# First norm's factor moved to the outputs of the query, key and value projections, rotary swap by DMA

## The chip, the cores and the metric

The kernel runs on one core of a Trainium2 chip. The metric is the device time of one execution in microseconds (us). The engines are TensorE (PE, with its weight loads PEld), VectorE (DVE), ScalarE (ACT), GpSimd (POOL) and SyncE (SP). ACT and SP also issue DMAs, each on a queue of its own.

## The reference

The program is a chain of four cross-attention layers on x of 8 batches x 112 tokens x 512. All that concerns this change is the start of layer 0: an RMS norm, query, key and value projections with two sets of weights that a token mask chooses between, rotary position encoding, and self-attention in 16 heads of 32.

```
xn = ln_in_w * (x * rsqrt(mean(x*x) + 1e-6))
m  = (type[t] == 1) & (type[t+1] == 1)             # 0 for the last token
qkv = m * (xn @ v_qkv) + (1 - m) * (xn @ l_qkv)    # [.., 1536]
rotate_half(u) = concat(-u[16:32], u[0:16])        # within each head of 32
q, k = u * cos[pos] + rotate_half(u) * sin[pos]    # for u = q, k
self-attention (causal), dense, residual; cross-attention, gated MLP, and three more layers
```

A factor that belongs to one token can be put behind a projection, since the projection sums over features only.

## The kernel before

Activations are kept transposed, 128 features in the partitions by tokens in the columns; the 896 tokens are two halves of 448 (`HALF`), and 512 features are four blocks (`KD`). A float32 product is made of three passes in the fast format float32r: high by high, high by low and low by high. So each weight chunk of 128x1024 is loaded by SP into `raw` (3 slots), and split by GpSimd into `wh` (one copy) and `wl` (four subtractions), in 4 slots. A chunk of the stage `qk` holds the v and the l weights of one output block m, and there are 16 tiles in `RAW`'s order: half 0 with m 0 to 3, half 1 with m 0 to 3, then the same with m 4 to 7. m below 4 is q, above is k. One tile is 24 matmuls, 12 into each of two PSUM banks (`e` = 0 for v, 1 for l weights). A slot of `wh` is free once half 1's tile has used it.

The order of work on each engine is written out by hand. Each engine walks through `SEQ["qk"]`: norm steps `("norm", nn, half, part)`, the table step and the tiles. `PoolPlan` gives each PE tile a PSUM bank from a rotating list (3 banks before), and PE waits for the bank's last reader.

The head: ACT squares x (L998), DVE sums the squares into `total` (L1289, L1292), PE multiplies by 1/512 (L618), ACT takes the root (L1003), DVE the reciprocal (L1316) and x times weight times factor (L1331), ACT rounds that to `nh` (L1015), DVE subtracts to get `nl` (L1338). PE makes the cos and sin tables by a one-hot product (L628). The half 1 norm is hooked behind tile 0 (`s`) and tile 1 (`v`, `f`).

A tile's way out: DVE multiplies each bank by its mask and scale (L1529, twice), adds the two (L1562). PE then makes the swapped copy by a float32 matmul with `rot_w` (L913, two passes), one tile later. DVE's `rope` multiplies raw by cos (L1545), the swapped bank by sin (L1548), and adds (L1551). Behind the 16th tile PE computes the values projection of batch 0 (L874 to L876); ACT waits for all 16 ropes before it scales that (L1123), and DVE adds its part (L1412); then attention starts with scores (L802) and masked minimum (L1434).

Of the kernel before, what the change touches and what calls it, by code (L numbers as in the profile page):

```python
# [29 lines left out]
F32 = mybir.dt.float32  # L30
# [7 lines left out]
P = 128  # L38
SCRATCH = 1024
B, S, D = 8, 112, 512  # L40
T = B * S
# [112 lines left out]
LATE = (1, 2)  # L154
# [57 lines left out]
def build(nc, xT, ctxF, ctxK, kmask, tt, ttT, pos, walls, vecs, gates, consts, outT):  # L212
    ctx = ExitStack()
    with ctx:
# [50 lines left out]
        ctxt = at("ctxt", [P, 4, CH * CC], F32, o_k)  # L265
        rt = at("rt", [P, T], F32, o_k)
        vr2 = at("vr2", [P, 2, HALF], F32, o_k + 4 * T)
        place[0] = max(place[0], o_k + 4 * 4 * CH * CC)
# [35 lines left out]
        eps = sb("eps", [P, 2])  # L304
        o_a = place[0]
# [45 lines left out]
        raw_qk = sem("raw_qk")  # L351
        tile_ready = sem("tile_ready")
# [27 lines left out]
        gated = sem("gated")  # L380
        normed = sem("normed")
# [73 lines left out]
        def both(*hooks):  # L455
# [7 lines left out]
            "qk": [("norm", 0, 0, "s"), ("norm", 0, 0, "v"), ("table",), ("norm", 0, 0, "f")] + qk_order(parts(0, 1, s=(0, 0, 0), v=(0, 0, 1), f=(0, 0, 1))),  # L463
# [17 lines left out]
        for name in SEQ:  # L481
            for it in SEQ[name]:
                if it[0] == "norm" and it[3] in ("a", "s", "s0", "x", "x0"):
# [69 lines left out]

        block = ctx.enter_context(nc.Block())
# [3 lines left out]
        def _(pe):  # L558
# [49 lines left out]
            def norm_part(nn, half, part):  # L608
# [6 lines left out]
                elif part == "v":  # L615
                    n = begin_tile(("var", nn, half), "act")
                    pe.wait_ge(summed_up, sum_no[nn, half, "v"])
                    nc.tensor.matmul(pool_bank(n)[:, 0:HALF], mean_w, total[:, :], start=True, stop=True)\  # L618
                        .then_inc(tile_ready, 1)

            qk_seen = [0]
# [9 lines left out]
            def stage(name, rhs_of, nblocks, who, mpc, ready=None, nn=None, items=None, only=None):  # L631
# [10 lines left out]
                for j in items or range(len(seq)):  # L642
# [261 lines left out]
            pe.wait_ge(cst_in, 16)  # L904

            def nhl(half, i):
                return nh_[:, i, hcols(half)], nl_[:, i, hcols(half)]

            def rotate(i):

                pe.wait_ge(raw_qk, i + 1)
                n = begin_tile(("rot", i), "dve")
                nc.tensor.matmul(pool_bank(n)[:, 0:HALF], rot_w, scr[:, i % 2, :],  # L913
                                 start=True, stop=True).then_inc(tile_ready, 1)

# [5 lines left out]

            stage("qk", nhl, KD, ("dve", "dve"), 1, nn=0)
            rotate(len(RAW) - 1)


# [3 lines left out]

            attention(att_self)  # L930
# [32 lines left out]
        def _(act):  # L963
# [10 lines left out]
            def norm_part(nn, half, part):  # L974
# [24 lines left out]
                elif part == "v":  # L999
                    bank = empty(("var", nn, half))  # L1000
                    if turn_of[nn, half] >= 1:
                        act.wait_ge(std_used, turn_of[nn, half])
                    nc.scalar.activation(std[:, :], bank[:, 0:HALF], ACT.Sqrt,  # L1003
                                         bias=eps[:, 0:1] if e == 1e-6 else eps[:, 1:2]).then_inc(emptied["act"], 1)
# [13 lines left out]
            def stage(name, each):  # L1018
                for it in SEQ[name]:
                    if it[0] == "norm":  # L1020
                        norm_part(*it[1:])
                    elif it[0] == "table":
                        for i, dst in enumerate((cosT, sinT)):
                            bank = empty(("table", i))
                            nc.scalar.copy(dst[:, :], bank[:, 0:S]).then_inc(emptied["act"], 1)
# [79 lines left out]
            for half in range(2):  # L1105
                act.dma_start(x[:, :, hcols(half)], xT[:, :, hcols(half)]).then_inc(x_in[half], 16)
# [6 lines left out]
            act.wait_ge(vmT_done, 2)  # L1113
# [109 lines left out]
        def _(dve):  # L1223
# [22 lines left out]
            def norm_part(nn, half, part):  # L1246
# [13 lines left out]
                elif part in X_PART:  # L1260

                    if part in ("x", "x0"):
# [3 lines left out]
                    for k in X_PART[part]:  # L1266
# [3 lines left out]
                            .then_inc(normed, 1)  # L1270
                        dve.wait_ge(sq_ready, i + k + 1)
# [6 lines left out]
                    if part in ("x", "x3"):  # L1278
# [24 lines left out]
                elif part[0] in "rf" and nn in LATE:  # L1303
                    tile_done(dve, ("var", nn, half))
                    own = rt[:, cols] if nn == 2 else rstd[:, :]
# [612 lines left out]
```

## Time and profile before

| what | value |
|---|---|
| median of 3 runs | 2025.97 us (2022.82 to 2027.89) |
| profiled execution | 2026.49 us, its span 2024.5 us |
| PE busy | 1915.1 us, 95% |
| DVE busy | 1131.6 us, 56% |
| ACT busy | 831.1 us, 41% |
| POOL busy | 883.7 us, 44% |
| chain of waits | PE 82%, DVE 7%, POOL 5%, ACT 2%, issue 2% |
| DMA to landing, weight chunk of 512 KB | 3.6 us (median) |
| DMA sizes at the start | x 896 KB a half, constants 383.5 KB, token types 448 KB, positions 49 KB, vectors 26 KB |

Shares are averages over stages with different limits. The rows give start and duration in us from the span's start; a bracket at the end of a row is idle time of the engine before it and what ended it. `x4` at the end of a timeline row means that four alike were merged. The granted clock is a share of TensorE's full speed: 1.00 is 2.4 GHz, 0.50 is 1.2 GHz.

### The profile page before, as it was taken

What the parts mean: (1) busy time and instruction counts of PE and PEld (TensorE: products, weight loads), DVE (VectorE), ACT (ScalarE), POOL (GpSimd) and SP (SyncE); (2) the same over time, 40 slices, a digit from 0 to 9 for tenths busy, and PEclk for the clock granted to TensorE, in tenths of its full rate; (3) what the DMA queues carried; (4) which work ended last, traced back from release to release, by engine and by line L of the source; (5) the groups of instructions that cost most, each with busy time, mean ns of one, the idle gap of its engine ahead of it and who ended that gap; (6) DMA issues with size and microseconds to landing.
All of it is one profiled execution on the core that took longest, in us unless ns stands there. A gap on an engine that the chain in (4) does not pass through costs nothing.

```text
span 2024.5 us, 35457 instructions
## 1 busy us (share of the span) xinstructions
PE 1915.1 (95%) x12620; PEld 1643.0 (81%) x12620; DVE 1131.6 (56%) x2699; ACT 831.1 (41%) x2198; POOL 883.7 (44%) x1037
## 2 busy tenths in 40 slices
PE   4999989997999999999999999998979999999998
PEld 3776777776999989888988879985458988888997
DVE  6777866665543654547676554222384766655422
ACT  2017527884211211256666423222235666652321
POOL 3340313240888999642121338850044212104884
PEclk9999988998999999999999999999989999999999
DMA  3110100010333333310000123322221000001332
GB/s 127 42 58 2 40 16 17 30 54 3 96 113 106 114 114 115 98 35 18 10 24 12 55 76 105 105 83 88 76 75 35 18 10 24 13 1 42 105 115 78
DMA packets 38189, 118.87 MB, mean 59 GB/s; under 512 B 6168, under 2 KB 10264, under 8 KB 38016
## 3 DMA queue, kind: packets, MB, share of 16 engines
q1 hardware_dynamic: 31408, 107.92, 17.2%
q10 hardware_dynamic: 6608, 8.68, 1.4%
q8 instruction: 104, 1.70, 0.4%
q14 instruction: 69, 0.57, 0.1%
HBM read 114.75 MB, written 1.84 MB: 58 GB/s over the span
## 4 chain that ended last, share of the span: by engine, by line
PE 82%; DVE 7%; POOL 5%; ACT 2%; issue 2%; DMA 1%; DVEq 0%; ACTq 0%; SPq 0%; POOLq 0%
PE psum L580 15%; PE psum L582 14%; PE psum L581 14%; PE psum L802 7%; PE psum L813 6%; PE psum L860 5%; PE psum L573 4%; PE psum L700 4%; PE psum L702 4%; PE psum L701 4%; POOL wl L1760 3%; ACT probs_t L1067 1%; POOL wh L1752 1%; PE psum L874 1%; DVE rstd L1316 1%
## 5 line engine op out<-in xcount | busy, mean ns | idle before, releaser
L1760 POOL TENSOR_TENSOR wl<-raw,wh 128x256 fp32r<-128x256 f32 x656 | 512.5, 812 | 13.7
L1752 POOL TENSOR_SCALAR wh<-raw 128x1024 fp32r<-128x1024 f32 x164 | 189.5, 1155 | 402.0 <-PE psum L582 161.1
L580 PE MATMUL psum<-nh,wh 128*128 128x448 f32 x904 | 349.6, 387 | 14.2 <-DVEq L1531 5.3
L581 PE MATMUL psum<-nl,wh 128*128 128x448 f32 x904 | 337.0, 373 | 0.0
L582 PE MATMUL psum<-nh,wl 128*128 128x448 f32 x904 | 336.7, 372 | 0.0
L1067 ACT ACTIVATE probs_t<-masked_t,nmin 112x375 f32<-112x375 f32 (+1 forms) x384 | 202.6, 528 | 109.7 <-DVE nmin L1434 109.7
L1607 DVE TENSOR_TENSOR hid_l<-scr,hid_h 128x448 fp32r<-128x448 f32 x108 | 92.3, 855 | 227.7 <-ACT hid_h L1153 227.1
L580 PEld LDWEIGHTS psum<-nh,wh 128*128 128x128 f32 x904 | 175.0, 194 | 37.1 <-issue 13.3
L1434 DVE CUSTOM_DVE_ANT_0 masked_t<-psum,maskf 112x375 f32<-112x375 f32 x256 | 129.8, 545 | 116.6 <-PE psum L802 116.0
L1094 ACT COPY probsT_t<-psum 125x336 f32<-125x336 f32 (+1 forms) x424 | 175.4, 456 | 43.5 <-PE psum L860 24.3
L813 PE MATMUL psum<-cst,probs_t 112*125 112x112 f32 (+1 forms) x1304 | 189.7, 276 | 3.6 <-ACT probsT_t L1094 3.2
L581 PEld LDWEIGHTS psum<-nl,wh 128*128 128x128 f32 x904 | 175.0, 194 | 20.0 <-issue 5.5
L813 PEld LDWEIGHTS psum<-cst,probs_t 112*125 112x125 f32 (+1 forms) x1304 | 167.0, 186 | 25.5 <-issue 9.3
L582 PEld LDWEIGHTS psum<-nh,wl 128*128 128x128 f32 x904 | 174.2, 193 | 15.0
L1474 DVE TENSOR_SCALAR probs_t<-probs_t,rinv 112x376 f32<-112x376 f32 (+1 forms) x392 | 157.8, 444 | 7.2
L1752 POOL TENSOR_SCALAR ctxh<-raw 128x750 fp32r<-128x750 f32 x24 | 20.1, 837 | 324.2 <-PE psum L582 206.8
L700 PE MATMUL psum<-hid_h,wh 128*128 128x448 f32 x432 | 157.8, 365 | 0.0
L702 PE MATMUL psum<-hid_h,wl 128*128 128x448 f32 x432 | 157.2, 364 | 0.0
L701 PE MATMUL psum<-hid_l,wh 128*128 128x448 f32 x432 | 157.2, 364 | 0.0
L1053 ACT COPY v<-psum 125x512 f32<-125x512 f32 (+1 forms) x144 | 68.6, 477 | 124.0 <-PE psum L860 119.0
L1168 ACT ACTIVATE scr<-psum 128x448 f32<-128x448 f32 x64 | 34.9, 545 | 199.9 <-PE psum L582 184.8
L860 PE MATMUL psum<-probsT_t,v 125*64 125x112 f32 (+1 forms) x2304 | 113.5, 264 | 1.3 <-ACT probsT_t L1094 1.1
(192 smaller groups left out, 3874.1 us busy)
## 6 DMA issues: line engine op xcount, KB each, us to landing
raw<-in_walls SPq DMA_DIRECT2D x183, 512.0 KB, 3.6
raw<-in_ctxF SPq DMA_DIRECT2D x24, 375.0 KB, 3.0
ctxb<-in_ctxF ACTq DMA_DIRECT2D x8, 375.0 KB, 3.5
ctxt<-in_ctxK ACTq DMA_DIRECT2D x8, 375.0 KB
x<-in_xT ACTq DMA_DIRECT2D x2, 896.0 KB, 11.5
outT<-x SPq DMA_DIRECT2D x2, 896.0 KB, 5.1
mask<-in_kmask ACTq DMA_DIRECT2D x16, 41.0 KB, 2.6
vself<-in_tt SPq DMA_DIRECT2D x1, 448.0 KB, 6.8
```

Of the source, the lines that this page charges most:

```text
L580: nc.tensor.matmul(out, ah, bh, start=(i == 0), stop=False)
L581: nc.tensor.matmul(out, ah, bl, start=False, stop=False)
L582: last = nc.tensor.matmul(out, al, bh, start=False, stop=(i == n - 1))
L700: nc.tensor.matmul(out, w[0][:, blk], ah, start=(i == 0), stop=False)
L701: nc.tensor.matmul(out, w[0][:, blk], al, start=False, stop=False)
L702: last = nc.tensor.matmul(out, w[1][:, blk], ah, start=False, stop=(i == nt - 1))
L813: last = nc.tensor.transpose(t_bank(g)[0:a.kw, o:o + S], probs[s % NPROB][:, c * a.kw:(c + 1) * a.kw], ident[0:S, 0:S])
L860: last = nc.tensor.matmul(pv_bank[o:o + w, col * S:(col + 1) * S], v1[0:KEYS, slot, c, ov:ov + w], pT, start=(c == 0), stop=(c == CH - 1))
L1067: nc.scalar.activation(probs[s % NPROB][:, 0:a.nk], src, ACT.Exp, scale=-1.0, bias=nmin[:, s % NPROB:s % NPROB + 1], accum_out=total).then ...
L1094: nc.scalar.copy(probsT[g % NTURN][0:a.kw, 0:w], t_bank(g)[0:a.kw, 0:w]).then_inc(a.probs_out, 1)
L1752: nc.gpsimd.tensor_scalar(high, src, 1.0, 1.0, ALU.mult, ALU.mult).then_inc(split_h, 1)
L1760: last = nc.gpsimd.tensor_tensor(low[cut], src[cut], high[cut].bitcast(F32), ALU.subtract)
```

## The change

It does five things. (1) The order of the first loads: SP loads constants, positions and the first weight chunk, then the token types, and waits for x half 0 before it goes on; ACT issues x half 1 only when half 0 has landed. (2) The first norm joins the kind (`LATE`, part `x`) whose factor is applied later: ACT makes `nh` from x and its weight directly, DVE makes `nl`, and both are used unscaled. For half 0 PE sums the four squares itself, in PSUM, once over all partitions into every row, and once (with the squares as the stationary side, 2 columns wide) with the tokens in partitions. For half 1 DVE still sums, and PE makes both forms. (3) The factor: `vr0` = factor x mask, used at the two banks of each q and k tile; `rstd_t` in the other form goes into the masks `vmT` of the values. (4) The rotary swap is done by DMA: 8 transfers of 16 partitions by 448 columns per tile between raw and `turned_qk`, 4 issued by ACT, 4 by SP (`SWAPS` says behind which weight load). Raw has 4 slots and rope i comes behind tile i + 2. The sign goes into the sin table. (5) The stage has all 8 PSUM banks, and PE starts the scores of the first four batches when 12 ropes are done.

```
+SWAPS = {6: range(5), 7: (5,), 8: (6,), 9: (7,), 10: range(8, 13), 11: (13,), 12: (14,), 13: (15,)}
-LATE = (1, 2)
+LATE = (0, 1, 2)
...
-            "qk": [("norm", 0, 0, "s"), ("norm", 0, 0, "v"), ("table",), ("norm", 0, 0, "f")] + qk_order(parts(0, 1, s=(0, 0, 0), v=(0, 0, 1), f=(0, 0, 1))),
+            "qk": [("norm", 0, 0, "x"), ("norm", 0, 0, "v"), ("table",), ("norm", 0, 0, "f")] +
+            qk_order(parts(0, 1, x=(0, 0, 0), v=(0, 0, 2), f=(0, 0, 3))),
...
+        def raw_of(i):
+            return (scr, xc)[i % 4 // 2][:, i % 4, :]
+        def swap(i, j):
+            return turned_qk[16 * j:16 * j + 16, i % 2, :], raw_of(i)[16 * (j ^ 1):16 * (j ^ 1) + 16, :]
...  TensorE, part "v"
+                    if (nn, half) == (0, 0):
+                        for k in range(KD):
+                            pe.wait_ge(sq_ready, k + 1)
+                            first, stop, own = k == 0, k == KD - 1, sq[:, k % 2, :]
+                            nc.tensor.matmul(pool_bank(n)[:, 0:HALF], mean_w, own, start=first, stop=False)
+                            for j in range(BPH):
+                                last = nc.tensor.matmul(pool_bank(n)[0:S, HALF + 2 * j:HALF + 2 * j + 2], own[:, bcols(j)],
+                                                        mean_w[:, 0:2], start=False, stop=stop and j == BPH - 1)
+                            last.then_inc(sq_used, 1)
...
-                    if name == "qk":
-                        if qk_seen[0] >= 1:
-                            rotate(qk_seen[0] - 1)
-                        qk_seen[0] += 1
...
-                        pe.wait_ge(rope_done, 16)
+                        pe.wait_ge(rope_done, 12 if b < BPH else 16)
...
+            plan.use(range(8))
             stage("qk", nhl, KD, ("dve", "dve"), 1, nn=0)
-            rotate(len(RAW) - 1)
...
+            plan.use(range(POOL))
+            for bank in range(POOL, 8):
+                bank_free(bank)
             attention(att_self)
...  ScalarE
-            for half in range(2):
-                act.dma_start(x[:, :, hcols(half)], xT[:, :, hcols(half)]).then_inc(x_in[half], 16)
+            act.dma_start(x[:, :, hcols(0)], xT[:, :, hcols(0)]).then_inc(x_in[0], 16)
+            act.wait_ge(x_in[0], 16)
+            act.dma_start(x[:, :, hcols(1)], xT[:, :, hcols(1)]).then_inc(x_in[1], 16)
...
+            def rotate(half, m):
+                i = qk_seen[0]
+                qk_seen[0] += 1
+                act.wait_ge(raw_qk, i + 1)
+                if i >= 2:
+                    act.wait_ge(rope_done, i - 1)
+                for j in range(P // 32):
+                    act.dma_start(*swap(i, j)).then_inc(turned_in[i % 2], 16)
-            stage("qk", None)
+            stage("qk", rotate)
...  VectorE, part "f"
+                        nc.vector.reciprocal(rstd_t[:, hb], std_t[:, hb]).then_inc(std_t_used, 1)
                     nc.vector.reciprocal(own, std[:, :]).then_inc(std_used, 1)
+                        for e in range(2):
+                            nc.vector.tensor_mul(vmT[:, e, hb], vmT[:, e, hb], rstd_t[:, hb]).then_inc(vmT_done, 1)
+                        for e, v in enumerate((vm, vml)):
+                            n = link(nc.vector.tensor_mul(vr0[:, e, cols], rstd[:, :], v[:, half * BPH:(half + 1) * BPH, :]
...  VectorE, rope
                 link(nc.vector.tensor_mul(t, raw_t, cos))
-                dve.wait_ge(tile_ready, n + 1)
-                bank = pool_bank(n)[:, 0:HALF].rearrange("p (b s) -> p b s", b=BPH)
-                nc.vector.tensor_mul(dst, bank, sin).then_inc(emptied["dve"], 1)
-                nc.vector.tensor_add(dst, dst, t).then_inc(rope_done, 1)
+                dve.wait_ge(turned_in[i % 2], 16 * (P // 16) * (i // 2 + 1))
+                other = turned_qk[:, i % 2, :].rearrange("p (b s) -> p b s", b=BPH)
+                dve.wait_ge(chain, link(nc.vector.tensor_mul(dst, other, sin)))
+                nc.vector.tensor_sub(dst, t, dst).then_inc(rope_done, 1)
...  qk: -if i >= 1: rope(i - 1)   +if i >= 2: rope(i - 2), and rope of the last two behind the stage
...  SyncE
+            sp.dma_start(cst[:, :], consts).then_inc(cst_in, 16)
             sp.dma_start(scr[0:S, 3, 0:S].bitcast(I32), pos.partition_broadcast(S)).then_inc(pos_in, 16)
             for n, (use, name, c) in enumerate(USES):
+                if n == 1:
+                    sp.dma_start(vself[:, 0:T].bitcast(I32), tt.partition_broadcast(P)).then_inc(tt_in, 16)
+                    sp.dma_start(scr[0:S, 2, 2 * B:4 * B].bitcast(I32), ttT).then_inc(ttT_in, 16)
+                    sp.wait_ge(x_in[0], 16)
...  behind the load of use n
+                for i in SWAPS.get(n, ()):
+                    sp.wait_ge(raw_qk, i + 1)
+                    if i >= 2:
+                        sp.wait_ge(rope_done, i - 1)
+                    for j in range(P // 32, P // 16):
+                        sp.dma_start(*swap(i, j)).then_inc(turned_in[i % 2], 16)
```

## Rows read from the trace of the kernel before

**Rows 1.** Timeline, head: start, us, engine, line, output and input, [idle before, releaser]

```profile
1.19 1.30 ACTq L1106 DMA_DIRECT2D x<-in_xT  x2
...
2.53 1.02 ACTq L1107 DMA_DIRECT2D gate_in<-in_gates  x1
...
10.46 1.28 ACT L998 ACT_TABLE_LOAD   x1 [10.46 <-DMA x<-in_xT]
...
11.75 1.04 ACT L998 ACTIVATE sq<-x 128x448 f32<-128x448 f32 x2
12.26 3.24 POOL L1760 TENSOR_TENSOR wl<-raw,wh 128x256 fp32r<-128x256 f32 x4
...
13.30 0.64 DVE L1520 TENSOR_TENSOR vmT<-scr 112x8 f32<-112x8 f32 x1
...
18.62 1.83 PE L618 MATMUL psum<-total,cst 128*128 128x448 f32 x2 [18.62 <-DVEq L1296]
...
20.25 1.04 PE L628 MATMUL psum<-onehot,cst 112*128 112x112 f32 x4
...
20.49 0.64 ACT L1003 ACTIVATE std<-psum,eps 128x448 f32<-128x448 f32 x1 [2.54 <-PE psum L618]
...
21.16 2.95 DVE L1316 RECIPROCAL rstd<-std 128x448 f32<-128x448 f32 x1 [2.74 <-ACT std L1003]
```

**Rows 2.** The chain of waits: start, us, piece; two of twelve alike

```profile
80.28 0.75 PE psum L913 x2
86.00 0.75 PE psum L913 x2
```

**Rows 3.** Windows: stretch, busy us of PE to POOL, granted PE clock, DMA

```profile
50.00:55.00 5.00, 0.00 (x0) 0.00 (x0) 4.87 (x9) 3.40 (x5) 0.00 (x0) 0.95 0.00 0
...
58.00:61.00 3.00, 3.00 (x10) 2.65 (x9) 1.14 (x2) 0.00 (x0) 0.00 (x0) 0.50 0.00 0
```

**Rows 4.** Timeline where the projections end

```profile
138.01 1.22 DVE L1551 TENSOR_TENSOR kT<-kT,xc 128x448 f32<-128x448 f32 x1
...
140.79 0.27 DVE L1434 CUSTOM_DVE_ANT_0 masked_t<-psum,cst 112x112 f32<-112x112 f32 x1
```

**Rows 5.** DMA view of 0 to 60 us: GB/s in 40 slices of 1.5 us

```profile
GB/s 0 52 161 408 397 401 408 397 396 268 10 221 128 0 156 194 22 268 60 0 109 240 0 0 0 0 0 0 0 0 0 5 0 0 0 0 0 11 0 0
```

**Rows 6.** Timeline of DVE, one tile with GpSimd idle

```profile
97.46 0.62 DVE L1529 SCALAR_TENSOR_TENSOR scr<-psum,vml 128x448 f32<-128x448 f32 x1 [1.85 <-PE psum L582]
...
98.89 0.63 DVE L1545 TENSOR_TENSOR xc<-scr,cosT 128x448 f32<-128x448 f32 x1
99.43 0.62 DVE L1548 TENSOR_TENSOR kT<-psum,sinT 128x448 f32<-128x448 f32 x1
100.16 0.62 DVE L1551 TENSOR_TENSOR kT<-kT,xc 128x448 f32<-128x448 f32 x1
100.70 0.62 DVE L1529 SCALAR_TENSOR_TENSOR scr<-psum,vm 128x448 f32<-128x448 f32 x1
```

**Rows 7.** Source view of line 1036: ns min/median/max of one DMA issue

```profile
L1036 ACTq DMA_DIRECT2D mask<-in_kmask x16: 318/319/445, 475.4 to 1738.8; - x16
```

**Rows 8.** DMA view of the whole span: issues, KB each, median us to landing

```profile
mask<-in_kmask ACTq DMA_DIRECT2D x16, 41.0 KB, 2.6
...
gate_in<-in_gates ACTq DMA_DIRECT2D x1, 2.0 KB, 13.3
```

**Rows 9.** Timeline, one tile with GpSimd splitting weights

```profile
127.25 1.09 POOL L1752 TENSOR_SCALAR wh<-raw 128x1024 fp32r<-128x1024 f32 x1 [1.08 <-PE psum L913]
...
127.45 1.35 DVE L1545 TENSOR_TENSOR xc<-scr,cosT 128x448 f32<-128x448 f32 x1
...
128.42 3.45 POOL L1760 TENSOR_TENSOR wl<-raw,wh 128x256 fp32r<-128x256 f32 x4
...
128.73 0.61 DVE L1548 TENSOR_TENSOR kT<-psum,sinT 128x448 f32<-128x448 f32 x1
...
129.45 1.13 DVE L1551 TENSOR_TENSOR kT<-kT,xc 128x448 f32<-128x448 f32 x1
```

More of the change, by code:

```diff
@@ L351, in build @@
         raw_qk = sem("raw_qk")
+        turned_in = [sem(f"turned_in{i}") for i in range(2)]
+        sign_done = sem("sign_done")
         tile_ready = sem("tile_ready")
@@ L482, in build @@
             for it in SEQ[name]:
-                if it[0] == "norm" and it[3] in ("a", "s", "s0", "x", "x0"):
+                if it[0] == "norm" and it[3] in ("a", "s", "s0", "x", "x0") and it[1:3] != (0, 0):
                     what = "m" if it[3] == "a" else "v"
@@ L616, in norm_part @@
                     n = begin_tile(("var", nn, half), "act")
-                    pe.wait_ge(summed_up, sum_no[nn, half, "v"])
-                    nc.tensor.matmul(pool_bank(n)[:, 0:HALF], mean_w, total[:, :], start=True, stop=True)\
-                        .then_inc(tile_ready, 1)
-            qk_seen = [0]
+                    pe.wait_ge(cst_in, 16)
+                    if (nn, half) == (0, 0):
[7 more added lines that the diff above has]
+                            last.then_inc(sq_used, 1)
+                        pe.wait_ge(sq_used, KD)
+                        pe.sem_inc(tile_ready, 1)
+                        return
+                    pe.wait_ge(summed_up, sum_no[nn, half, "v"])
+                    last = nc.tensor.matmul(pool_bank(n)[:, 0:HALF], mean_w, total[:, :], start=True, stop=True)
+                    if nn == 0:
+                        for j in range(BPH):
+                            last = nc.tensor.matmul(pool_bank(n)[0:S, HALF + 2 * j:HALF + 2 * j + 2], total[:, bcols(j)],
+                                                    mean_w[:, 0:2], start=True, stop=True)
+                    last.then_inc(tile_ready, 1)
             def tables():
@@ L1024, in stage @@
                             bank = empty(("table", i))
-                            nc.scalar.copy(dst[:, :], bank[:, 0:S]).then_inc(emptied["act"], 1)
+                            if i:
+                                act.wait_ge(sign_done, 1)
+                            nc.scalar.activation(dst[:, :], bank[:, 0:S], ACT.Copy, scale=sign[:, 0:1] if i else 1.0)\
+                                .then_inc(emptied["act"], 1)
                     elif each:
@@ L1260, in norm_part @@
                 elif part in X_PART:
-                    if part in ("x", "x0"):
+                    if part in ("x", "x0") and (nn, half) != (0, 0):
                         sum_free(nn, half, "v")
@@ L1270, in norm_part @@
                             .then_inc(normed, 1)
+                        if (nn, half) == (0, 0):
+                            continue
                         dve.wait_ge(sq_ready, i + k + 1)
@@ L1277, in norm_part @@
                         ins.then_inc(sq_used, 1)
-                    if part in ("x", "x3"):
+                    if part in ("x", "x3") and (nn, half) != (0, 0):
                         dve.wait_ge(sq_used, i + KD)
@@ L1576, in dense @@
                         ins.then_inc(dense_done, 1)
-            stage("qk", qk)
+            stage("qk", qk, range(1, len(SEQ["qk"])))
+            rope(done[0] - 2)
             rope(done[0] - 1)
+            dve.wait_ge(vmT_done, 6)
             values(0, 1)
```

64 lines of the change are left out of this document (37 added, 27 removed).

## The prediction

> **What bounds the kernel now.** I read the page first: the matrix engine (PE) is busy in 95% of the span, and most of the chain of waits is PE work. All edited code that runs more than once lies before the first attention, so I then read only the first 142 us, by timeline, by waits, by windows and by the chain, in that order. The reader is to see there: (a) a head of some 26 us in which PE does almost nothing, because x arrives late, its squares are summed on the vector engine (DVE), and root, reciprocal, scaling and splitting follow each other [rows 1]; (b) 16 projection tiles, 5.71 us apart in the chain, of which 0.75 us is the rotary matmul pair [rows 2]; (c) one hole: PE runs nothing from 50 to 55 us and then has a granted clock of 0.50 up to 61 us, that is the 1.2 GHz level [rows 3]; (d) the end: the last rotary sum ends at 138.01 + 1.22 = 139.2, and attention's first masked score begins at 140.8 [rows 4]. Everything behind 140.8 keeps its code, so the change is worth what it moves that 140.8, less what it leaves behind.
>
> **The change part by part.** The sum follows DVE, since PE loses work and DVE loses little.
>
> 1. *x first.* Before, ACT's first work on x starts at 10.46, when half 0 has landed [rows 1]. By then the DMA moved 1.5 us x (52 + 161 + 408 + 397 + 401 + 408) GB/s = 2.74 MB [rows 5]. After, only 2.38 MB are issued ahead of x half 0's landing (x 0.92, vectors 0.03, constants 0.39, positions 0.05, one weight chunk 0.52, token types 0.47): 2.13 MB are through at 9.0, the rest takes 0.6 us. I take 9.7; bounds 8.4 (the two queues share evenly, 1.89 MB) and 10.5 (no gain). But ACT now waits before it issues x half 1 (0.65, half of the 1.30 of the pair) and the gates (1.02), then loads its table (1.28), makes nh (0.57) and the square (0.57, half of 1.04 and a start) [rows 1]: first square at 13.8. Before it was ready at 12.3.
>
> 2. *Squares summed by PE.* Each of four k-blocks takes the mean matmul on 448 columns (one pair took 1.83 with its tail, I take 1.5 at the low clock) and four small ones of 2 columns, each in two passes. The nearest row for a small one is the table's: four passes in 1.04 us with a tail of 0.4, so 0.21 each [rows 1]. That makes 1.5 + 8 x 0.21 = 3.2 us at 1.2 GHz, half of it, 1.6, at 2.4 GHz. In the trace PE had the low level for 6 us after it restarted [rows 3]: 3.2 + 3.0 + 1.6 + 1.6 = 9.4, and the variance is there at 23.2 (before: 20.45). Bounds: all at the high level 6.4 (20.2); all at the low level with 0.34 a pass, 16.8 (30.6). ACT would need only 1.15 us a block and stands behind PE through its two square buffers. A price of a page alone: the Trainium skill, "TensorE: Matmul & The Clock Gate", section "LDWEIGHTS (loading the stationary operand)", says that a load costs its columns over 1.2 GHz, which is 0.09 us for 112 columns at either clock; by it the small passes are 0.7 us a block and the variance would be some 2 us earlier. No row here shows a 2-column matmul.
>
> 3. *Factor at the outputs.* Root 0.64 and its small twin 0.25: 24.1. Then DVE: reciprocals 0.2 + 2.95, two small products 0.65 each beside GpSimd [rows 1], two products 0.7 each: 5.9, so 30.0. What goes is the scaling and splitting behind the reciprocal, which held PE's first tile until 33.8 and made the hole at 50. nh and nl are made from raw x at 13 to 19 us, beside PE's sums. With all 8 banks PE runs tiles 0 to 2 from 23.8 to 38.7 (5.71 - 0.75 = 4.96 each [rows 2]) without waiting for DVE.
>
> 4. *Half 1's norm.* DVE: first tile 2.2 (0.77 + 0.77 + 0.66, starts of the steps in [rows 6]), so raw 0 at 32.2. ACT stands at the swap: 4 issues at 0.32 [rows 7], 33.5; then 8 activations of 0.57, 38.1; DVE's last sum 38.8. PE arrives at 38.7 and waits next to nothing: no hole. Its sum is 0.75 + 0.8, tile 3 ends at 45.4, and tile 15 at 40.4 + 13 x 4.96 = 105. DVE: tiles 1 and 2 with rope 0 until 45.0, tile 3 with rope 1 until 49.4, factors of half 1 (4.8, GpSimd idle) until 54.2. ACT's root for half 1 comes behind swap 2, at about 47.6, in time.
>
> 5. *Swap by DMA.* PE loses 16 x 0.75 = 12.0 us. On DVE the product with sin read the PSUM bank and now reads SBUF. 8 issues a tile, 4 on each queue: 1.3 us; landing 2.6, the median of the masks' 41 KB [rows 8]: L = 3.9 from rope i-2 to data (bounds 2.9, if issues hide behind the landing, and 6.7, with issues at 1.02 as the gates'). DVE does two tiles in between, 6 us or more, so none of it shows but at the end. SP's weight loads are queued behind those waits: chunk 7 issues at about 65, lands by 69, and is wanted at 70. The Trainium skill, "DMA: Bandwidth & Descriptors", section "Issuing engines are not separate DMA queues", holds that a second queue only saves issue time; by it the split is worth the 1.3 us once, at the tail.
>
> 6. *DVE as the new bound.* Undisturbed a tile is from 97.46 to the end of the next first step, 3.9, so 4.0 us with its gap [rows 6]; PE needs 4.96. But while GpSimd splits weights, the product with cos took 1.35 instead of 0.63 and the sum 1.13 instead of 0.62, while the product that reads PSUM stayed at 0.61 [rows 9]. That product now becomes a third of the slow kind: 4.0 + 0.7 + 0.5 + 0.6 = 5.8 us a tile (bounds 5.2, no more than now, and 6.8, rival below). GpSimd splits four chunks (5.0 each) from PE's tile 4 end (50.4 to 70.4) and from tile 12's end (90.1), then context to 116. From 54.2: 12 x 4.0 = 48, plus 16.2 x (1 - 4.0/5.8) = 5.0 in the first window, plus 0.31 x (E - 90.1) in the second: E = 114.9 for tile 15 with rope 13. Swap 15 waits for rope 13: + 3.9, and 1.5 for rope 15: 120.3. The way from there to the first mask is 1.6 as now [rows 4]: 121.9 against 140.8, 18.9 us earlier.
>
> 7. *What is left behind.* PE has finished its values projection by 111 and idles some 10 us, so attention starts at the 1.2 GHz level. Six us at that level did the work of three [rows 3], so 3.0 at most; I take 2.7 as part of the start waits for DVE.
>
> Sum: -18.9 + 2.7 = -16.2. The profiled execution took 2026.5 (span 2024.5), the median of the runs is 2026.0. 2026.5 - 16.2 = 2010.3; I say 2010.
>
> **The rivals.**
> *PE stays the bound* (DVE is not slowed further by GpSimd). For: outside the splits DVE has 0.9 us a tile to spare. Against: [rows 9]. Tile 15 ends at 105.0, raw 15 at 107.2, rope 13 at 109.1, swap lands 113.0, first mask 116: 24.8 earlier, less 2.7: 2004.4.
> *The port is held whole.* If every DVE step with two SBUF inputs and every GpSimd step exclude each other, a tile and a chunk together cost 1.09 + 3.24 + 4 x 0.62 = 6.8 us for both [rows 1, 6, 9]. A window of four is then 27 us, 11 over the undisturbed 16, twice 22, where my sum holds 13: 9 later, 2019. For: the copy to wh starts beside DVE's product and both are long in [rows 9]. Against: before, 4.88 of GpSimd and three such steps fitted in 5.71 us. This is the rule of the Trainium skill, "SBUF — State Buffer", section "SBUF: two separate sides" (whoever starts first holds the shared pair for its whole instruction), and it speaks against this change, since that moves an input from PSUM into SBUF. The trace agrees in kind, with 1.35 against 0.63, not in full size.
> *The sums stay at the low clock.* The variance comes at 30.6 and DVE's line moves by 7.4: 2017.7.
> *The swap is the bound (the other side).* Rope i waits for a DMA that waits for rope i-2, so two tiles cannot take less than L + 1.4. It decides from L = 11: from rope 3 at 62, six pairs of 12.4 end at 136.4, which with 2.7 for the cold start is no gain. The gates' transfer landed 13.3 us after its issue behind x [rows 8]; with L = 13 it is 12 us slower, 2038. Against: nothing bulky is on ACT's queue then, and on SP's one 512 KB load.
> *The change does little*: x no earlier, the head's gain spent, 2021 to 2026.
>
> **How the numbers follow.** Forecast 0.47, PE-bound 0.15, port held whole 0.13, low clock 0.14, swap-bound 0.05, little 0.06. The low ones' shares end at 2003, the two slow ones' at 2020, so I give 2002 to 2021 for 8 in 10. 0.3% is 6 us, what a measurement here can tell from no change. Faster by more (below 2020): 0.47 + 0.15 + 0.08 + 0.12 and a bit = 0.84. Within: 0.09. Slower: 0.07, the swap and a share of what I did not see.
>
> **What would show it.** Right: no idle stretch of PE between tile 2 and tile 4, tiles 4.96 apart; the sin product at about 1.1 beside GpSimd; first square near 13.8 and root near 23.5; first mask near 122 with PE idle 8 to 12 us before it. Wrong: DVE waiting for the swap DMAs before its sin products in mid-stage (swap-bound); PE's low clock past 25 us; first mask at 116 or at 130 (the port rivals); or time lost behind 141, where I expect none but the cold start.

## The result and the profile after

The changed kernel takes 2028.24 us (median of 20 runs, 2023.84 to 2033.15) against 2025.43 (20 runs of the kernel before, 2021.35 to 2031.32): ratio 1.0017, 95% interval 1.0009 to 1.0024. That is inside the bound of 0.3%, on the slow side of no change by 0.09 to 0.24%; I had forecast 2010. Its profiled execution took 2030.77 (span 2029.0), which is 4.3 more than the 2026.49 of the one before.

Where the time went, by landmarks of the two traces:

| landmark | before | after | difference |
|---|---|---|---|
| first root (std) | 20.5 | 27.3 | +6.8 |
| first masked score starts | 140.79 | 128.43 | -12.4 |
| last masked score of the first attention starts | 254.73 | 252.60 | -2.1 |
| end of the execution | 2026.5 | 2030.8 | +4.3 |

So the head did gain, though 12.4 and not 18.9 us; 10.3 of it were gone by the end of the first attention, and 6.4 more were lost in stages whose code is the same in both.

The timeline of the head, after. These lines answer to [rows 1] and, for the swap, to [rows 7]; the columns are the same.

```profile
14.24 0.56 ACT L1010 ACTIVATE sq<-x 128x448 f32<-128x448 f32 x1
...
14.94 1.83 PE L643 MATMUL psum<-sq,cst 128*128 128x448 f32 x2 [14.94 <-ACT sq L1010]
...
16.57 1.52 PE L645 MATMUL psum<-cst,sq 128*112 128x2 f32 x8
...
25.61 1.52 PE L645 MATMUL psum<-cst,sq 128*112 128x2 f32 x8
...
27.26 0.63 ACT L1028 ACTIVATE std<-psum,eps 128x448 f32<-128x448 f32 x1 [4.24 <-PEq L649]
...
29.01 0.57 PE L610 MATMUL psum<-nh,wh 128*128 128x448 f32 x1
...
29.39 0.57 PE L611 MATMUL psum<-nh,wl 128*128 128x448 f32 x1
...
32.48 0.36 PE L601 MATMUL psum<-nl,wh 128*128 128x448 f32 x1
...
32.69 0.36 PE L602 MATMUL psum<-nh,wl 128*128 128x448 f32 x1
...
36.34 2.81 ACTq L1153 DMA_DIRECT2D turned_qk<-scr  x4
...
40.08 0.68 DVE L1313 SCALAR_TENSOR_TENSOR nl<-x,vec,nh 128x448 fp32r<-128x448 f32 x1 [3.77 <-ACT nh L1006]
```

The reader is to see that PE's sums (L643, L645) come every 3.0 us from 14.94 to 27.1, the fourth no faster than the first, and that four issues of the swap take ACT 2.81 us, behind which DVE waits 3.77 us for half 1's `nh`. The window view gives a granted clock of 1.00 for 14 to 32 us, but the pace contradicts it: matmuls of 448 columns start 0.38 us apart at 29 us and 0.21 at 32.5, and half 1's sum takes 0.99 us for the pair and 0.86 for the eight small passes, where half 0's blocks take 1.83 and 1.52. So I read PE's pace up to about 31.5 us as that of the low level.

Windows of after that answer to [rows 3]:

```profile
36.00:50.00 14.00, 13.92 (x72) 12.34 (x71) 9.41 (x17) 4.22 (x8) 0.00 (x0) 1.00 0.13 30
50.00:55.00 5.00, 5.00 (x26) 4.64 (x25) 4.60 (x10) 0.79 (x2) 0.00 (x0) 1.00 0.24 55
```

The hole of before at 50 to 55 is gone: PE is busy in all of it, at a granted clock of 1.00.

The end of the projections, which answers to [rows 4, 6, 9]:

```profile
118.50 1.27 DVE L1609 TENSOR_TENSOR kT<-turned_qk,sinT 128x448 f32<-128x448 f32 x1
...
120.50 2.40 SPq L1851 DMA_DIRECT2D turned_qk<-xc  x4
120.52 2.68 ACTq L1153 DMA_DIRECT2D turned_qk<-xc  x4
...
122.57 1.39 DVE L1606 TENSOR_TENSOR xc<-xc,cosT 128x448 f32<-128x448 f32 x1
...
124.56 0.62 DVE L1609 TENSOR_TENSOR kT<-turned_qk,sinT 128x448 f32<-128x448 f32 x1 [0.60 <-DMA turned_qk<-xc]
125.22 0.62 DVE L1610 TENSOR_TENSOR kT<-xc,kT 128x448 f32<-128x448 f32 x1
125.92 0.69 ACT L1168 ACTIVATE vtmp<-psum,vmT 112x512 f32<-112x512 f32 x1 [1.19 <-issue]
126.76 0.75 DVE L1472 SCALAR_TENSOR_TENSOR vself<-psum,vmT,vtmp 112x512 f32<-112x512 f32 x1 [0.92 <-ACT vtmp L1168]
127.72 0.72 PE L834 MATMUL psum<-kT,qT 32*112 32x112 f32 x4 [9.97 <-DVE vself L1472]
...
128.43 0.27 DVE L1494 CUSTOM_DVE_ANT_0 masked_t<-psum,cst 112x112 f32<-112x112 f32 x1 [0.92 <-PE psum L834]
```

DVE is now the bound, its product with sin (L1609) takes 1.27 beside GpSimd's subtractions and 0.62 for the last tile, and PE stands idle for 9.97 us. Behind the last rotary sum there is a step that I had not seen: the first scores wait for the emptying of the values' bank (L1168, L1472).

Windows of after behind that hole, and of before in the same place:

```profile
115.00:120.00 5.00, 1.93 (x6) 0.97 (x6) 4.64 (x7) 0.00 (x0) 4.20 (x4) 0.70 0.40 92
120.00:125.00 5.00, 0.00 (x0) 0.00 (x0) 4.37 (x6) 1.49 (x2) 3.45 (x3) 0.50 0.39 107
...
130.00:140.00 10.00, 10.00 (x38) 6.15 (x42) 4.08 (x28) 4.51 (x18) 0.00 (x0) 0.50 0.00 0
140.00:150.00 10.00, 10.00 (x49) 6.17 (x46) 4.56 (x31) 3.93 (x16) 0.00 (x0) 0.50 0.00 0
150.00:160.00 10.00, 10.00 (x79) 6.41 (x78) 7.35 (x45) 6.49 (x28) 0.00 (x0) 0.94 0.01 2
```

```profile
130.00:140.00 10.00, 9.26 (x41) 6.32 (x39) 8.21 (x10) 0.68 (x1) 9.08 (x10) 1.00 0.20 55
140.00:150.00 10.00, 9.69 (x66) 6.19 (x63) 7.99 (x48) 6.90 (x31) 3.47 (x5) 1.00 0.42 144
150.00:160.00 10.00, 10.00 (x85) 6.52 (x87) 7.98 (x50) 6.88 (x30) 0.00 (x0) 1.00 0.01 2
```

After, the clock is at 0.50, the 1.2 GHz level, up to about 150 us. PE counts as busy all the time, but runs 38 and 49 matmuls in 10 us where the kernel before runs 66 to 85. That is the loss inside the first attention. For the loss behind it no window shows a cause: in stretches of 200 to 400 us from 260 on, the granted clock is the same in both (0.95 to 0.99), and PE is busy for nearly the same share.

### The profile page after: what moved, and what is told of

Same layout as the page of the kernel before. It is cut to its first block, busy times and chain, and to the rows that moved or that the text cites. A ratio compares the mean times of both kernels' runs of the same rounds, so it can differ in the third digit from the quotient of the medians.

```text
span 2029.0 us, 35606 instructions
## 1 busy us (share of the span) xinstructions
PE 1923.1 (95%) x12634; PEld 1645.7 (81%) x12634; DVE 1130.6 (56%) x2698; ACT 831.1 (41%) x2200; POOL 882.7 (44%) x1037
## 4 chain that ended last, share of the span: by engine, by line
PE 78%; DVE 8%; POOL 7%; issue 4%; ACT 2%; DMA 2%; ACTq 0%; DVEq 0%; POOLq 0%
PE psum L600 14%; PE psum L601 12%; PE psum L602 12%; PE psum L834 7%; PE psum L845 6%; PE psum L892 5%; PE psum L593 4%; POOL wl L1821 4%; PE psum L732 4%; PE psum L733 4%; PE psum L734 4%; POOL wh L1813 1%; ACT probs_t L1099 1%; PE psum L906 1%; POOL kvwl L1821 1%
## 5 line engine op out<-in xcount | busy, mean ns | idle before, releaser
L600 PE MATMUL psum<-nh,wh 128*128 128x448 f32 x904 | 343.9, 380 | 7.8 <-POOL wl L1821 4.0
L845 PEld LDWEIGHTS psum<-cst,probs_t 112*125 112x125 f32 (+1 forms) x1304 | 167.2, 186 | 27.3 <-issue 10.0
```

The lines of the kernel that those rows point to most:

```text
L600: nc.tensor.matmul(out, ah, bh, start=(i == 0), stop=False)
L845: last = nc.tensor.transpose(t_bank(g)[0:a.kw, o:o + S], probs[s % NPROB][:, c * a.kw:(c + 1) * a.kw], ident[0:S, 0:S])
```

## The experiments

Of each edit the deciding lines are shown, and the comments behind # are mine. All times are medians of runs on one chip, beside runs of the kernel before on the same chip; "first" and "last" are the starts of the first and last masked score of the first attention in the profiled execution (before 140.8 and 254.7).

### The cold start

**e1_warm**: the changed kernel with unread work for PE in the hole.

```
+            bank_free(6)
+            for _ in range(46):
+                nc.tensor.matmul(psum[:, 6, 0:HALF], nh_[:, 0, 0:P], nh_[:, 0, 0:HALF], start=True, stop=True)
```

> The changed kernel with 46 matmuls of 448 columns whose result nobody reads, run by PE in the hole between the values projection (ends near 118 us) and the first scores (near 128). Theory A, the cold start ate the gain: the first mask stays at 128.4, the granted clock stays at 1.00 through the first attention, its end moves from 2 us to about 12 us ahead of the kernel before, and the median falls by about 10 us, to 2017 to 2019. Rival B, the time is lost behind attention by something that the change altered there: the first attention ends earlier, but the total stays near 2028. Rival C, attention waits for something else than PE's clock: first attention as slow as before, median 2028.

Measured: 2025.01 (12 runs; before 2025.05), ratio 1.0002, 0.9990 to 1.0013. First 128.8, last 244.5. Its windows, which stand against those of after above:

```profile
130.00:140.00 10.00, 10.00 (x62) 6.36 (x64) 6.45 (x44) 6.29 (x27) 0.00 (x0) 0.83 0.00 0
140.00:150.00 10.00, 10.00 (x89) 6.54 (x88) 7.92 (x50) 6.92 (x30) 0.00 (x0) 1.00 0.01 2
```

The low clock was the loss inside the attention: 8.1 us of it come back in the trace. But the end of the span comes only 2.1 us earlier and the median falls by 3 us only, not by the 10 expected, and this is where a second cause had to be looked for. The granted clock, averaged over an execution, says that the profiled execution of after was on the bad side, too: 0.973 there, 0.9747 on average over its 20 runs, 0.9792 with the unread matmuls and 0.9800 before.

**e4_idle**: the kernel before with the hole alone.

```
+            for _ in range(14):
+                dve.wait_ge(chain, link(nc.vector.tensor_add(xc[:, 2, :], xc[:, 2, :], xc[:, 3, :])))
```

> The kernel before with 14 dependent additions on DVE (about 10 us) between its last rope and the scaled values, so that PE gets a hole of 10 us ahead of attention as in the changed kernel. Theory A: the 10 us are paid twice, once as delay and once as slow clock in attention: median 2043 to 2048. Rival, a cold start is over after some 6 us as it was at 55 us in the kernel before: delay plus 3, median 2038 to 2040.

Measured: 2041.38 (6 runs), ratio 1.0082, 1.0061 to 1.0102: 16.3 us for a delay of 9.6. First 150.4 (+9.6), last 273.7 (+19.0). The windows of this kernel behind its hole:

```profile
140.00:150.00 10.00, 0.00 (x0) 0.00 (x0) 9.55 (x14) 0.00 (x0) 3.22 (x3) 0.57 0.35 105
150.00:160.00 10.00, 9.05 (x32) 5.71 (x33) 4.87 (x33) 5.15 (x21) 0.00 (x0) 0.50 0.00 1
160.00:180.00 20.00, 20.00 (x123) 12.42 (x122) 11.06 (x71) 9.61 (x40) 0.00 (x0) 0.70 0.01 1
```

So an idle PE ahead of the first attention costs 9.4 us in a trace and some 7 in the median, with nothing of the change in it. The forecast had 2.7 for it.

**e2_early** (the values' banks taken from the low end of the pool, so that the first scores don't wait for their emptying) and **e5_quiet** (the low parts of chunks 4 to 11 left out but for one piece in four, so that GpSimd works less).

```
 e2  +            plan.use(range(POOL))          # ahead of the values, not behind them
 e5  +                if u[1] in ("qk", "v") and RING_NO[u] >= RING:
     +                    pieces = pieces[:1]
```

> The changed kernel with the values projection of batch 0 in banks 0 to 1, so that PE waits only for tiles' banks, not for the scaled values, before its first scores. Theory A: the first mask comes 0.9 us earlier (127.5), PE has scores and three values matmuls to do in the hole but is still idle over 5 us, the clock still falls, and the median stays at 2026 to 2028. Rival: the few matmuls in the hole are enough to keep the clock, and the median falls by 8 us or more.

> The changed kernel with three of GpSimd's four subtractions left out for the eight weight chunks 4 to 11 (those low parts are then stale). Theory, DVE is slowed by GpSimd's work on the same port: DVE's steps with two SBUF inputs are 0.62 in most of tiles 4 to 15, DVE falls to 4.0 us a tile and then to PE's 4.9, and the first mask comes at about 119 to 121 instead of 128.4. Rival, the slow steps are slow for another reason (the swap DMAs writing SBUF): they stay above 1.0 and the first mask stays within 1 us of 128.4.

Measured: e2_early 2026.86 (12 runs), ratio 1.0018, 0.9999 to 1.0036; first 128.0, last 243.9. Two of these runs were far off, 2045.46 and 2064.21 at mean granted clocks of 0.967 and 0.955, and the ratio leaves out the second. e5_quiet 2012.56 in its one run; first 124.2, last 240.1. So GpSimd's subtractions beside DVE are worth 4.2 us of the head and not the 7 to 9 expected: 13 of the 16 products with sin took 0.61 to 0.62 us, though the swap's DMAs ran as before, and two of the three slow ones (1.23) stood beside the splitting of the context, which this edit left in.

The traces with a hole ahead of attention can be laid side by side. "Low" is the time at 0.50 from 115 us on (a window's mean clock below 1.00 read as a share of it at 0.50), and then the part of it behind the first masked score, with PE at work:

| kernel | PE idle ahead of the first scores | low | low behind the first mask | first to last mask |
|---|---|---|---|---|
| before | 0.3 | 0 | 0 | 113.9 |
| after | 10.0 | 34 | 23 | 124.2 |
| e4_idle | 11.6 | 31 | 22 | 123.3 |
| e9_align (below) | 10.3 | 17 | 11 | 119.1 |
| e7_dvesum (below) | 9.7 | 20 | 9 | 118.1 |
| e2_early | 9.8 | 10 | 5 | 115.9 |
| e5_quiet | 7.7 | 7 | 4 | 115.9 |
| e1_warm | 1.0 | 3 | 3 | 115.7 |

Attention is longer than before by about half of the low time behind its first mask, as it must be if PE bounds it and goes at half pace. And behind much the same hole the low level lasts very unlike times. That is how one execution can lose 10 us and the median 3.

**v1_ahead, v2_ahead_warm**: real work in the hole, the values projection of batch 1, with each later one moved up by a batch (v1), and 18 unread matmuls beside it (v2).

```
-                            if a is att_self and s % 2 == 0 and s // NH + 1 < B:
-                                values(s // NH + 1, s % NH // 8, s % 8 // 2)
+                            if a is att_self and s % 2 == 0 and s // NH + 2 < B:
+                                values(s // NH + 2, s % NH // 8, s % 8 // 2)
```

> The changed kernel with the values projection of batch 1 (24 matmuls, 5.5 us) moved from the first attention into the hole ahead of it, every later batch's one batch earlier. Theory A: PE's hole shrinks to 4 to 5 us, attention loses 5.5 us of PE work, and whether the clock falls decides between a median near 2012 (kept) and 2022 (fallen). Rival, attention is not bound by PE: median within 2 us of 2028.

> As the one with batch 1's values ahead, and 18 matmuls of 448 columns that nobody reads (3.7 us) in what is left of the hole. Theory A: the granted clock stays at 1.00, first attention ends 15 us ahead of the kernel before (about 240 us), median 2010 to 2013. Rival as above.

Measured: 2026.22 and 2026.22 (12 runs each; before 2026.75), ratios 1.0006 (0.9991 to 1.0021) and 1.0000 (0.9987 to 1.0013), so neither gave the gain expected. First 129.4 and 128.8, last 251.8 and 247.2. The work moved up is missing at the end of the attention, where a new hole took the clock to 0.79 between 200 and 240.

### The head

**e6_peswap** (the swap back on PE, two tiles behind) and **e7_dvesum** (half 0's squares summed by DVE again).

```
 e6  +                        if qk_seen[0] >= 2:
     +                            rotate(qk_seen[0] - 2)
 e7  -                    if part in ("x", "x0") and (nn, half) != (0, 0):
     +                    if part in ("x", "x0"):
```

> The changed kernel with the rotary swap made by PE again (two passes a tile, two tiles behind, sin product read from PSUM), all else kept. Theory: PE's tiles are 5.7 us apart again and PE sets the end of the stage, DVE is not slower than PE: tile 15 ends at about 117 to 120 and the first mask at about 128 to 131, PE's hole is under 5 us, so the clock mostly stays and the median is 2013 to 2020, better than with the DMA swap. Rival, the swap by DMA is what gave the 12 us: first mask at 134 or later, and no gain in the median against the changed kernel.

> The changed kernel with half 0's squares summed by DVE again (copy and three additions), PE making one product of the sum. Theory: DVE's sum ends near 20 us (it now also makes nl, beside GpSimd), the root comes at about 22.5 instead of 27.3, and everything on DVE's line, the first mask too, moves 3 to 5 us earlier, to 123.5 to 125.5. Rival, DVE's steps delay each other and the root comes no earlier: first mask within 1 us of 128.4.

Measured: e6_peswap 2031.6 (10 runs), ratio 1.0029, 1.0013 to 1.0045; first 132.7, between what the theory and its rival foresaw and 4.3 later than after: that is what the swap by DMA gains in the head. e7_dvesum 2028.21 in its one run, root at 27.5, first 129.3: PE's slow sums cost nothing against DVE's, and what I expected of them fell.

### The loss behind the attention

In the dense stages I took the mean time from start to start of three matmuls in succession (high x high, low x high, high x low, each on 448 columns). Three on the hidden tiles (hid_h, hid_l) took 603 ns in the kernel before and 608 in the changed one; in stretches of tens of us, in nearly every kernel (v3 has none over 8 us), all triples took 620. The change allocates three small tiles ahead of probs_t, and hid_h and hid_l, which share its bytes, move by 96.

**e9_align** (those tiles behind probs_t), **e10_before_shift** (96 unused bytes in the kernel before) and **v3_warm_align** (e9 with the matmuls of e1):

```
 e9   -        sign = sb("sign", [P, 1])
      -        std_t = sb("std_t", [S, B])
      -        rstd_t = sb("rstd_t", [S, B])
               o_a = place[0]
...
               probs_t = sb("probs_t", [S, NPROB, 376])
      +        sign = sb("sign", [P, 1])
      +        std_t = sb("std_t", [S, B])
      +        rstd_t = sb("rstd_t", [S, B])
 e10  +        place[0] += 96
               o_a = place[0]
```

> The changed kernel with its three new small tiles (sign, std_t, rstd_t, 96 bytes in all) allocated behind the probabilities, so that probs_t, hid_h and hid_l lie at the byte offsets that they had before (hid_h at 217120, which is 32 above a multiple of 64; in the changed kernel it is at 217216, a multiple of 64). Nothing else is changed. Theory A (the offset sets part of the pace of the feed-forward matmuls): three matmuls on hid_h and hid_l take 601 ns from start to start again, as before the change, not 608; 432 such triples make some 3 us, and with fewer slow stretches of the others 3 to 9 us; time 2017 to 2024, faster than the kernel before by 0.1 to 0.4%. Rival B (placement of data has no part, the pace of a run is drawn): the triples on hid stay at 608 or fall where they fall in any run, and the time is that of the changed kernel, 2026 to 2029.

> The kernel before with 96 unused bytes ahead of probs_t, hid_h and hid_l, and nothing else: they lie where the changed kernel has them. Theory A: its triples on hid_h and hid_l go from 601 to 608 ns and it is 3 to 9 us slower than the kernel before, 2028 to 2034. Rival B: no difference from the kernel before, 2024 to 2027.

> The changed kernel with both: 46 unread matmuls in the hole ahead of the first scores, and the offsets of before. Theory A (offset) with theory of the clock: the head of the kernel gains 10 us up to the end of the first attention, the stages behind run as before the change: 2014 to 2019. Rival B: as the version with the unread matmuls alone, 2024 to 2026.

**v4_nh_odd** and then, to take its two moves apart and to find what counts, **x1_all32**, **x2_probs96**, **x3_hid96** and **x4_nh32**, all from v3:

```
 v4  +        place[0] += 32        # ahead of nh; and 32 more behind nl
 x1  -        place = [SCRATCH + 128]
     +        place = [SCRATCH + 160]    # ahead of every tile
 x2  +        place[0] += 96        # ahead of probs_t, hid_h and hid_l kept
 x3  +        place[0] += 64        # ahead of probs_t, hid_h and hid_l
 x4  +        place[0] += 32        # ahead of nh; and 96 more behind nl
```

> The version before this one with nh and nl moved as well by 32 bytes, from a multiple of 64 to 32 above one; hid_h and hid_l stay 32 above one. Theory A in its wider form (any matmul operand read at 32 above a multiple of 64 goes at the faster pace): the triples on nh and nl go from 608 to about 601 ns; there are 904 of them with x 448 at 128 by 128, and more in the first projections, so some 6 to 8 us less than the version before this one, 2006 to 2012. Rival B: no effect of the offset, same as the version before this one. Rival C (it is not the offset modulo 64 but that the two are unlike in it, or the distance from the weights): nh triples change some other way, the hid ones too.

> The changed kernel with the unread matmuls and the offsets of before (v3), and every tile in SBUF moved up by 32 bytes: all distances stay, each offset changes from a multiple of 64 to 32 above one or the other way (hid_h is now at a multiple of 64, nh, nl and both rings of weights 32 above one). Theory R (what counts is how the operand stands to the weights): triples as in v3, 601 ns on hid, 607.5 on nh; 2016. Theory S (each operand's own offset counts, a multiple of 64 being dearer for the feed-forward's): hid at 608, 2020 or more; by what v4_nh_odd showed, nh and hid at 613 to 616 is also possible: 2025.

> v3 with probs_t alone moved up by 96 bytes, to where the changed kernel has it; hid_h and hid_l stay. Theory hid (the feed-forward's operands are the cost): triples on hid 601 ns, time that of v3, 2016. Theory probs (what the transposes read and VectorE and ScalarE write is the cost): 4 to 8 us more, 2020 to 2024.

> v3 with probs_t, hid_h and hid_l moved up by 64 bytes: 96 above a multiple of 128 in place of 32, and still 32 above a multiple of 64. If the offset counts modulo 64: triples on hid 601 ns and 2016, as v3. If modulo 128: 608 or the 613 of v4_nh_odd, and 2020 to 2025.

> v3 with nh and nl moved to 32 above a multiple of 128, hid_h and hid_l kept at 32 above one, too (all behind nl moves by 128 bytes). If the cost of v4_nh_odd came from nh and nl: nh triples at 616 again in place of 607.5, 2023 to 2026. If it came from hid's 96 modulo 128: nh triples at 601 to 608, 2008 to 2017.

Measured. Offsets are those of nh and of hid_h less that of the weights, modulo 128; triples are means in ns over some 65 to 87 each, good to about 1 ns, in the stretches 1212 to 1308 / 1884 to 1992 us. x1 to x4 ran beside 31 runs of the kernel before with a median of 2024.6; each ratio is to the runs on its own chip.

| kernel | nh, hid | hid triple | nh triple | median, runs | ratio, interval |
|---|---|---|---|---|---|
| before | 0, 32 | 603 / 602 | 607 / 608 | 2025.4, 25 | 1 |
| after | 0, 0 | 617 / 609 | 617 / 608 | 2028.2, 20 | 1.0017, 1.0009-1.0024 |
| e10_before_shift | 0, 0 | 608 / 614 | 609 / 614 | 2029.9, 8 | 1.0027, 1.0015-1.0039 |
| e9_align | 0, 32 | 619 / 601 | 618 / 608 | 2020.2, 12 | 0.9980, 0.9969-0.9992 |
| v3_warm_align | 0, 32 | 602 / 601 | 608 / 607 | 2016.2, 5 | 0.9961, 0.9947-0.9976 |
| x1_all32 | 0, 32 | 601 / 601 | 608 / 608 | 2018.9, 7 | 0.9971, 0.9959-0.9983 |
| x2_probs96 | 0, 32 | 608 / 602 | 611 / 607 | 2018.8, 12 | 0.9973, 0.9961-0.9984 |
| x3_hid96 | 0, 96 | 613 / 613 | 619 / 620 | 2026.0, 11 | 1.0007, 0.9996-1.0018 |
| v4_nh_odd | 32, 96 | 613 / 613 | 616 / 617 | 2025.8, 11 | 1.0004, 0.9994-1.0014 |
| x4_nh32 | 32, 32 | 620 / 620 | 620 / 620 | 2025.9, 11 | 1.0006, 0.9993-1.0020 |

Single starts have steps of 0.01 us, so a mean over many is needed, but the ends of the scale can be seen in four of them. Timelines of PE, first v3, then x4:

```profile
1949.75 0.36 PE L732 MATMUL psum<-hid_h,wh 128*128 128x448 f32 x1
...
1950.35 0.36 PE L732 MATMUL psum<-hid_h,wh 128*128 128x448 f32 x1
...
1950.95 0.36 PE L732 MATMUL psum<-hid_h,wh 128*128 128x448 f32 x1
...
1951.55 0.36 PE L600 MATMUL psum<-nh,wh 128*128 128x448 f32 x1
```

```profile
1949.75 0.37 PE L734 MATMUL psum<-hid_h,wh 128*128 128x448 f32 x1
...
1950.37 0.37 PE L734 MATMUL psum<-hid_h,wh 128*128 128x448 f32 x1
...
1950.99 0.37 PE L734 MATMUL psum<-hid_h,wh 128*128 128x448 f32 x1
...
1951.61 0.37 PE L602 MATMUL psum<-nh,wh 128*128 128x448 f32 x1
```

What follows:

- Placement is a cause, shown from both sides: 96 bytes added to the kernel before cost 0.27% (5.5 us), the same 96 bytes taken from the changed one give 0.37% (7.5 us), and 0.41% (8.3 us) with the unread matmuls in.
- The cost is mostly the hidden tiles': with probs_t alone moved (x2) their triple stays at 602 in the stretch without the 620 pace, and the ratio goes from v3's 0.9961 to 0.9973 (2.4 us, intervals overlap). Where hid_h and hid_l are moved as well (e1) it is 1.0002, 5.9 us more, and these intervals don't overlap.
- It is the distance from the other tiles and not the offset itself: with all of them moved by 32 bytes (x1), where hid_h is at a multiple of 64 as in after, the triples are those of v3.
- The pace of the matmuls is most of what is lost. Over all matmuls of 448 columns behind the first attention that follow each other without a gap (some 3,900), the mean from start to start is 202.9 ns before and 204.3 after, which makes 5.6 of the 6.6 us that the profiled execution of after takes longer there; 202.4 in v3 and 204.4 in e1 make 7.8 of 13.1 us. What the rest is, no trace shows.
- The 7 ns of the hidden tiles' 432 triples (608 instead of 601) are 3.0 us of that. The rest is the 620 pace, which comes and goes by stretches even with the placement of before (e9 at 1212 to 1308). Of the triples behind 260 us, 4 to 25% took 617 ns or more in the six kernels with hid_h and hid_l where they lay before (before, e4, e9, v3, x1, x2), 19 to 70% in the nine that have them 96 bytes on, and 80% in x4. So it is commoner with the moved tiles, but the ranges overlap, and what starts such a stretch is not shown.
- From the last mask of the first attention to the end, those six took 1768 to 1772 us, six of the nine 1775 to 1782, and three of the nine (e5, v1, v2) 1771 as well. So one execution alone doesn't tell the two placements apart; the ratios over many runs do.
- The wider theory, that an operand at 32 above a multiple of 64 goes faster, fell: with nh there everything ran at 613 to 620. No rule by one tile's distance fits, since x3 moves only probs_t and hid_h/hid_l and slows the triples on nh as well. That rule stays open.

The Trainium skill, "TensorE: Matmul & The Clock Gate", section "Wait — 56ns, not 53.3ns?", gives matmuls back to back at 2.4 GHz the time of their columns at that rate and about 2.5 ns; an estimate from it for a triple of 448 columns is 568 ns. The traces here don't agree for these operands: 601 at best, 620 at worst.

**v3_warm_align** beats both kernels: 0.39% faster than the kernel before (0.24 to 0.53, 5 runs), last masked score at 245.1.

## Why the prediction was wrong, step by step

*What bounds the kernel*: right in the head, and wrong in its last sentence. "Everything behind 140.8 keeps its code, so the change is worth what it moves that 140.8" took equal code for equal time. The same instructions on tiles moved by 96 bytes were 5.5 us slower (e10). This is the step that failed with the largest share of the error (7.5 us by e9 against after, 5.5 by e10). None of my rivals covered it, though time lost behind 141 was named as a sign of being wrong.

*Step 1, x first*: the first square started at 14.24, foreseen 13.8. Right.

*Step 2, the sums by PE*: 12.2 us for four blocks, foreseen 9.4. I let the clock rise after 6 us because it had done so in [rows 3]; there PE ran big matmuls end to end, here it had small ones and pauses, and stayed at the low pace to the end. A block at that pace was sized rightly (3.0 us, foreseen 3.2), and at the high pace too (half 1's pair and eight passes took 1.5 us from start to start, foreseen 1.6); only the rise was wrong. A small pass took 0.19 us at the low pace and 0.11 at the high one, not 0.09 at both, as the price taken from the page alone had it. The root came at 27.26, 3.8 late. It was inside the stated bounds, and e7 shows that the other way of summing is not sooner.

*Steps 3 and 4, factor at the outputs, half 1's norm*: right in kind (no hole, no wait of PE between tiles 2 and 4); the factors of half 1 were done at 59.4, foreseen 54.2, which is the lateness of step 2 (3.8) and of the issues in step 5: ACT's four took 2.81 us where 1.3 were foreseen, and DVE stood idle for 3.77 us up to 40.08 until ACT had made `nh`.

*Step 5, the swap*: landing 1.9 to 2.1 us (medians) instead of 2.6, but an issue 0.59 (SP) and 0.62 us (ACT), up to 0.88, instead of 0.32. I took the price of an issue from transfers out of HBM [rows 7]; these go from SBUF to SBUF; whether that makes the difference is not shown. That L came out near (4.1 at the last swap, foreseen 3.9) is luck, since both errors cancel in it, and DVE waited for a swap once, 0.60 us. The swap-bound rival was rightly low, and against e6 the swap by DMA is worth 4.3 us.

*Step 6, DVE as the bound*: right. The product with sin took 1.15 to 1.46 with GpSimd at work all through it, a tile 5.9 to 6.3 us (foreseen 5.8) and 3.93 without (4.0). But the rival "the port is held whole" is nearer to the truth than its chance of 0.13. From 62.8 to 72 us the two engines take turns: GpSimd's subtractions start 0.9 to 1.1 us apart, where they start 0.69 apart with DVE idle (four take 2.77 at 21.56), and DVE's steps with two SBUF inputs start 1.0 to 1.3 apart, where they start 0.54 to 0.66 apart with GpSimd idle. One of each takes about 1.1 us, little less than the 1.2 to 1.35 that full exclusion would take. The rival's 6.8 us for a tile and a chunk was too dear because its 3.24 for the subtractions was no undisturbed time; with 2.77 it is 6.3, and the traces show 6.0 for a tile and 5.3 for a chunk. The last rotary sum ended at 125.8 instead of 120.3: 5.2 of the 5.5 stood already at the start of this step. The way from there to the first mask was 2.6 and not 1.6, for the values' bank. So -12.4 in place of -18.9.

*Step 7, the cold start*: undersized, and the reason given doesn't carry over. "Six us at that level did the work of three" is true of the projections' long matmuls end to end. At the start of attention, among many short ones, the low level lasted 4 to 23 us behind the first mask where PE had stood idle for 8 to 12; what ends it is not shown. That cost 10.3 us and not 2.7 in the profiled execution, 9.4 in e4's and 2.0 in e2's and e5's, so the 2.7 lies within the spread. In the median the unread matmuls win back 3.0 (after to e1) and 3.8 (e9 to v3); the intervals of each pair overlap, so the size is rough. e4's median gives some 7.

Sum of the error, from -16.2 forecast to +3.4 measured (0.17% of 2025), 19.6 us: 6.5 for the later first mask, 7.5 for the placement, and for the clock, beyond the 2.7 in the forecast, some 0.3 to 1.1 by the unread matmuls and 4 by e4. That leaves 1.6 to 5.3 us open, which the intervals of the medians (2 to 3 us to each side of a difference) can hold in part; that this rest is noise is not shown.

## What to carry to other kernels

A tile added anywhere in SBUF moves every tile allocated behind it, so a change is to be compared with the old placement restored: here 96 bytes hid a gain of 0.2%. And when PE is relieved until it waits for another engine, part of the gain is paid back in clock: a hole of 10 us ahead of attention's short matmuls cost 3 to 7 us in the median, and between 2 and 10 in one execution.

## What was unexpected of the hardware

- Three fp32r matmuls in a row on 448 columns took 601, 608, 613 or 620 ns at the full granted clock, by how the tiles lay to each other in SBUF and, between 608 and 620, by the stretch. The medians of v3, v4 and x1 to x4 range from 2016.2 to 2026.0 with the same instructions.
- Behind a hole of PE of the same 10 us the granted clock was at 0.50 for 10, 17, 20 or 34 us (e2_early, e9_align, e7_dvesum, after).
- An issue of a DMA of 16 partitions from SBUF to SBUF took 0.59 (SP) or 0.62 us (ACT) in the median, twice that of a mask from HBM (0.32).
- DVE's steps with two SBUF inputs and GpSimd's subtractions took turns: one of each in 1.1 us, where they start 0.54 to 0.66 and 0.69 apart alone.
